# Cross-attention block: turning the attention probabilities through DRAM instead of on TensorE, with a deeper software pipeline

## The chip, the cores and the metric

One core of one Trainium2 chip runs the whole program. The metric is the time of one execution on the device in microseconds. The engines are PE (TensorE), DVE (VectorE), ACT (ScalarE), POOL (GpSimd) and SP (SyncE, which here only issues DMAs); each works through its own list of instructions in order and waits on semaphores that other engines raise.

## What is computed

64 batches, each with `x` and `ctx` of 128 x 512 in float32. A first attention works over channels (128) and positions (512), a second one has 16 heads of 32 channels over 128 queries and 128 keys, and a two-layer MLP follows. Cut to what matters:

```python
def _L0(x_c, x_s, Wn, bn, Wm, bm, Wl, bl, Wo, bo):
    Mn = _conv1x1(Wn, bn, _inorm(x_c)); Mm = _conv1x1(Wm, bm, _inorm(x_s))
    A = softmax(einsum('bct,bcs->bts', Mn, Mm), axis=-1)          # 512 x 512 per batch
    Mo = einsum('bcs,bts->bct', _conv1x1(Wl, bl, x_s), A)
    return _conv1x1(Wo, bo, Mo) + x_c
def _L1(h, enc, mask, ...):
    x = layer_norm(h, ln1_w, ln1_b)
    q, k, v = heads(x @ q_w + q_b), heads(enc @ k_w + k_b), heads(enc @ v_w + v_b)
    attn = softmax(where(mask, einsum('bhqd,bhkd->bhqk', q, k) * scale, min), axis=-1)
    hidden = merge(einsum('bhqk,bhkd->bhqd', attn, v)) @ cproj_w + cproj_b + h
    y = gelu(layer_norm(hidden, ln2_w, ln2_b) @ fc_w + fc_b) @ proj_w + proj_b
    return hidden + y
```

## The kernel before

The program has two passes. `attention_pass` computes both attentions and writes `hidden` to DRAM; `mlp_pass` then reads it. The change touches the first pass only.

Every float32 product is done in three passes of float32r (`three_passes`): each operand is split into an upper half (`..._hi`, by ACT or DVE) and a lower half (`..._lo`, a subtraction on DVE or POOL).

`attention_pass` is a software pipeline in *slots*. In slot `s` each engine runs `slot(s)`, which works on several batches at once: `b0` is batch s, `b1` batch s-1, and so on, and `ahead` batch s+1. Slots -1 to 5 and the last ones are written out; those between run in a loop of four slots a turn (`slots`, L389). The order of work on an engine is the order in which its `slot` is written, by hand, and so is the PSUM bank of each product (L376 to L384). Nothing is scheduled by a program.

What one slot does before, by the names used below, in PE's order (L922 to L1043):

- M (2 x 3 products of 512 columns): the two 1x1 convolutions of b0. A turn: 16 transposes of 128 x 128 (`turn`, L900) of the first attention's matrix of b1.
- QK half 0, S0 (scores of the first attention, b0), QK half 1. QK is the keys' projection in even slots and the queries' in odd ones, for a pair of batches (`project_pair`).
- U (b1); then the **probabilities' turn**: 16 transposes of the second attention's probabilities of b4, `probs[:, r, c, :]` into banks 2 to 5 (L995); ACT copies the four banks to `pT` (L630).
- OUT0 (b1), whose result with the residual becomes `x1` on DVE (L811); S1, the masked scores of the second attention (b3, L1016 and L1021); PV, values times `pT` (b4, L1029); V (b1); XN, four transposes of `x1n` (b1); C, the output projection (b4), which DVE adds to `x1b` as `hid` (L848).

Beside PE: DVE takes maxima and sums (L745, L762, L741), lower halves (L713, L751) and the biases of `kT` and `qT` (L727, L734). ACT takes exponentials (L609, L641) and copies. POOL normalises the probabilities (L567) and takes small powers and lower halves (L547 to L560). SP issues all DMAs in its own order (L465 to L493), each behind the wait written ahead of it; `blocks` is `ctx` loaded in four pieces to 32 partitions each, so that DVE's transpose of 32 x 32 blocks (L787) gives the full transpose of `ctx`.

Of the kernel before, what the change touches and what calls it, by code (L numbers as in the profile page):

```python
# [18 lines left out]
ALU = mybir.AluOpType  # L19
# [74 lines left out]
class Handover:  # L94
# [6 lines left out]
    def __init__(self, nc, stack):  # L101
# [20 lines left out]
        self.hid = sb("hid", [P, 2, 512])  # L122
# [65 lines left out]
def attention_pass(nc, x, ctx, mask, w, hidden, mlp):  # L188
# [8 lines left out]
    with ExitStack() as stack:  # L197
# [13 lines left out]
        probs = mlp.rows[:, 1, :, :].rearrange("p r (c n) -> p r c n", n=P)  # L211
# [11 lines left out]
        x_ctx_in = sb("x_ctx_in", [P, 2, 2, T])  # L223
        x_in, ctx_in = x_ctx_in[:, 0, :, :], x_ctx_in[:, 1, :, :]
# [3 lines left out]
        normed = sb("normed", [P, 2, T])  # L228
# [12 lines left out]
        x1n = sb("x1n", [P, D])  # L241
# [6 lines left out]
        mlp_raw = (x_ctx_in[:].rearrange("p s u t -> p (s u) t"),  # L248
# [90 lines left out]
        qT_set = sem("qT_set")  # L339
        k_done = sem("k_done")  # L340
        kT_set = sem("kT_set")
# [8 lines left out]
        pT_turned = sem("pT_turned")  # L350
        pT_copied = sem("pT_copied")
# [24 lines left out]
        M_BANK = (4, 5)  # L376
        AT_BANK = S1_BANK = (0, 1, 2, 3)
        QK_BANK = (6, 1)
        S0_BANK = (4, 5, 7, 0)
        U_BANK = XN_BANK = 6  # L380
        PT_BANK = (2, 3, 4, 5)
        OUT0_BANK = C_BANK = 7
        PV_BANK = 4
        V_BANK = 5  # L384

        FIRST, LOOPED, LAST = -1, 6, B + 3
# [29 lines left out]
        def _(sp):  # L416
# [5 lines left out]
            def load(e):  # L422
                if e.has_before(2):
                    after(normed_set, (e + -2).nth(2, 2))
                u = e.parity
                sp.dma_start(x_in[:, u, :], x[e.number]).then_inc(x_loaded[u], 16)
                sp.dma_start(ctx_in[:, u, :], ctx[e.number]).then_inc(ctx_loaded[u], 16)
# [24 lines left out]
            for i, n in enumerate(("bn", "bm", "bl", "bo")):  # L452
                sp.dma_start(bias0[:, i:i + 1], w[n].rearrange("(p a) -> p a", a=1)).then_inc(small_in, 16)
            load(Batch(0, 1, B))
            load_weight(K_W)
# [8 lines left out]

            def slot(s):  # L465
                e = s + 2
                if e.exists() and e.has_before(2):
                    load(e)
# [7 lines left out]
                e = s + -2  # L476
# [8 lines left out]
                if s.first():  # L485
                    load_weight(C_W)
                e = s + 1
                if e.exists() and e.has_before(1):
                    load_blocks(e)
                e = s + -4  # L490
                if e.exists():
                    after(hid_set, e.nth(1, 1))
# [24 lines left out]
        def _(pool):  # L517
# [14 lines left out]
            def slot(s):  # L532
# [8 lines left out]
                if b0.first():  # L541
                    lower_halves(K_W)
# [830 lines left out]
```

## Time and profile before

| | us |
|---|---|
| median of 3 runs (3113.08 to 3116.71) | 3116.62 |
| the profiled execution's own time | 3114.79 |
| its span, first to last instruction | 3112.8 |
| attention pass, to the last `hid` | some 1704 of it |
| one slot in the middle of the pass | 25.23, and 25.4 to 25.5 on the mean of four |

The profiled execution took 2 us outside its span, and it lies 1.8 us below the median. The MLP pass (the rest) is the same code in both kernels. The timeline views are read as follows: the start in us from the span's start, how long the row's instructions took together, the engine, the line of the kernel and the operation, what was written from what, and how many instructions are merged; in square brackets, how long the engine stood idle before it and whose end it then followed. Successive instructions of DVE and ACT overlap by some 0.06 to 0.1 us, so the distance of two starts, not the duration, is what an instruction takes of its engine.

### The profile page before, as it was taken

The numbers are of one execution on the slowest core, as the hardware profiler recorded it, in microseconds if no ns is written. First come the engines' busy times: TensorE is split into PE (matmuls) and PEld (weight loads), VectorE is DVE, ScalarE is ACT, GpSimd is POOL, SyncE is SP. The second block draws the span as 40 slices with busy tenths as digits, with TensorE's granted clock in tenths as the row PEclk, the third lists the DMA queues.
The fourth block names the chain that finished last, engine by engine and source line by source line (L and its number), as shares of the span: only waits on it lengthen the run. The fifth ranks groups of instructions, "written<-read, shape, count | busy, mean of one in ns | idle before, by whom it ended". The sixth has DMA issues, their size and how long they took to land. (4 is left out here: it accounts for less than half of the span.)

```text
span 3112.8 us, 56124 instructions
## 1 busy us (share of the span) xinstructions
PE 3043.9 (98%) x19575; PEld 2582.9 (83%) x19575; DVE 1802.5 (58%) x3577; ACT 1499.1 (48%) x4210; POOL 796.0 (26%) x742
## 2 busy tenths in 40 slices
PE   6999999999999999999996999999999999999999
PEld 5888888888888888888885888888888888888887
DVE  6777777777777777777774433333333333333332
ACT  5777777777777777777774211111111111111111
POOL 4444444444444444444433100000000000000000
PEclk8999999999999999999998999999999999999999
DMA  4111111111111111111102211111110111111110
GB/s 129 45 52 56 52 52 52 52 53 55 52 52 52 52 52 52 52 52 56 58 32 81 85 31 38 40 40 40 40 40 14 40 35 33 40 40 40 40 27 14
DMA packets 232040, 149.49 MB, mean 48 GB/s; under 512 B 142912, under 2 KB 176192, under 8 KB 231872
## 3 DMA queue, kind: packets, MB, share of 16 engines
q1 hardware_dynamic: 231872, 146.91, 16.0%
q8 instruction: 147, 2.41, 0.3%
q14 instruction: 21, 0.17, 0.0%
HBM read 97.57 MB, written 33.55 MB: 42 GB/s over the span
## 5 line engine op out<-in xcount | busy, mean ns | idle before, releaser
L1218 ACT ACTIVATE gl<-pre,fc_bias 128x512 f32<-128x512 f32 x256 | 176.6, 690 | 1119.9 <-PE pre L1303 1119.9
L1257 DVE CAST hT_hi<-gl 128x512 fp32r<-128x512 f32 x256 | 109.1, 426 | 839.5 <-ACT gl L1218 839.5
L641 ACT ACTIVATE rows<-bank,negmax 128x128 f32<-128x128 f32 x1024 | 359.4, 404 | 10.2 <-DVE negmax L745 10.2
L1301 PE MATMUL pre<-yT_lo,rest_hi 128*128 128x512 f32 x768 | 298.8, 389 | 0.0
L1302 PE MATMUL pre<-yT_hi,rest_lo 128*128 128x512 f32 x768 | 298.8, 389 | 0.0
L1303 PE MATMUL pre<-yT_hi,rest_hi 128*128 128x512 f32 x768 | 298.8, 389 | 0.0
L1301 PE MATMUL acc<-rest_lo,hT_hi 128*128 128x512 f32 x768 | 298.8, 389 | 0.0
L1302 PE MATMUL acc<-rest_hi,hT_lo 128*128 128x512 f32 x768 | 298.8, 389 | 0.0
L1303 PE MATMUL acc<-rest_hi,hT_hi 128*128 128x512 f32 x768 | 298.8, 389 | 0.0
L567 POOL TENSOR_TENSOR rows<-rows,rsum 128x512 f32<-128x512 f32 x256 | 261.4, 1042 | 90.0 <-DVE rsum L741 89.2
L609 ACT ACTIVATE rows<-bank,negmax 128x512 f32<-128x512 f32 x256 | 175.0, 688 | 213.0 <-DVE negmax L762 213.0
L641 ACT ACTIVATION_READ_ACCUMULATOR rows<-bank,negmax 128x1 f32 x1024 | 250.0, 244 | 0.0
L900 PEld LDWEIGHTS bank<-ident,rows 128*128 128x128 f32 x2048 | 231.5, 140 | 20.0 <-ACT rows L641 2.6
L900 PE MATMUL bank<-ident,rows 128*128 128x128 f32 x2048 | 245.2, 273 | 2.4 <-ACT rows L641 1.8
L177 POOL TENSOR_TENSOR rstd<-ve,neghalf 128x4 f32<-128x4 f32 x16 | 16.3, 1019 | 870.0 <-DVE ve L171 870.0
L615 ACT ACTIVATE rows<-rows,rsum 128x512 f32<-128x512 f32 x256 | 164.2, 713 | 69.6 <-DVE rsum L781 69.6
L1259 DVE TENSOR_TENSOR hT_lo<-gl,hT_hi 128x512 fp32r<-128x512 f32 x256 | 177.4, 693 | 8.8
L762 DVE TENSOR_REDUCE negmax<-bank 128x1 f32<-128x512 f32 x256 | 174.8, 691 | 2.6 <-PE bank L871 2.3
L547 POOL TENSOR_TENSOR in_rstd<-in_ve,neghalf 128x2 f32<-128x2 f32 x64 | 45.3, 708 | 510.6 <-DVE in_ve L776 510.6
L560 POOL TENSOR_TENSOR normed_lo<-normed,normed_hi 128x512 fp32r<-128x512 f32 x128 | 174.5, 1385 | 2.7 <-ACT normed_hi L635 2.7
L1302 PEld LDWEIGHTS pre<-yT_hi,rest_lo 128*128 128x128 f32 x768 | 144.3, 188 | 30.1
L1301 PEld LDWEIGHTS acc<-rest_lo,hT_hi 128*128 128x128 f32 x768 | 144.4, 188 | 29.9
(160 smaller groups left out, 7926.7 us busy)
## 6 DMA issues: line engine op xcount, KB each, us to landing
x_ctx_in<-in_x SPq DMA_DIRECT2D x64, 256.0 KB, 2.6
x_ctx_in<-in_ctx SPq DMA_DIRECT2D x64, 256.0 KB, 2.9
blocks<-in_ctx SPq DMA_DIRECT2D x256, 64.0 KB, 1.9
small<-in_x SPq DMA_DIRECT2D x64, 256.0 KB, 3.5
hidden<-hid SPq DMA_DIRECT2D x64, 256.0 KB, 2.0
rows<-hidden SPq DMA_DIRECT2D x16, 1024.0 KB, 5.5
out<-rows SPq DMA_DIRECT2D x64, 256.0 KB, 2.1
stage<-y SPq DMA_DIRECT2D x240, 64.0 KB, 2.1
```

Of the source, the lines that this page charges most:

```text
L560: pool.tensor_tensor(normed_lo[:, i, :], normed[:, i, :], normed_hi[:, i, :].bitcast(F32), ALU.subtract).then_inc(normed_lo_set, 1)
L567: pool.tensor_tensor(probs[:, r, :, :], probs[:, r, :, :], rsum1[:, r, :].unsqueeze(2).to_broadcast([P, 4, P]), ALU.mult).then_inc(probs_s ...
L609: act.activation(A_cols[:, t, :, :, :], bank[S0_BANK[t]][:].rearrange("p (d c x) -> p d c x", d=4, x=32), ACT.Exp, bias=negmax0[:, t:t + 1 ...
L615: act.activation(A[:, t, :], A[:, t, :], ACT.Identity, scale=rsum0[:, t:t + 1]).then_inc(a_scaled, 1)
L641: act.activation(probs[:, r, c, :], by_chunk(S1_BANK[r])[:, c, :], ACT.Exp, bias=negmax1[:, r, c:c + 1], accum_out=sum1[:, r, c:c + 1]).th ...
L762: dve.tensor_reduce(negmax0[:, t:t + 1], bank[S0_BANK[t]][:], AX_X, ALU.max, negate=True).then_inc(max0_set, 1)
L900: last = pe.transpose(out[:, c * P:(c + 1) * P], src(c), ident[:])
L1218: act.activation(gl[:, i % 2, :], pre[i % 2][:], ACT.Gelu_apprx_tanh, bias=mlp.fc_bias[:, i:i + 1]).then_inc(gelu_done, 1)
L1259: dve.tensor_tensor(hT_lo[:, i % 2, :], gl[:, i % 2, :], hT_hi[:, i % 2, :].bitcast(F32), ALU.subtract).then_inc(hT_lo_set, 1)
L1301: pe.matmul(out, a_hi, b_lo, start=first, stop=False)
L1302: pe.matmul(out, a_lo, b_hi, start=False, stop=False)
L1303: return pe.matmul(out, a_hi, b_hi, start=False, stop=last)
```

## The change

- The probabilities' turn leaves PE. The 16 transposes and ACT's four copies are gone. ACT's exponentials write `probs` in another order of columns: first the block `d` of 32 keys, then head row `r`, chunk `c` and the key within the block. POOL normalises one `r` at a time, in two calls of two.
- SP writes `probs` to a DRAM tensor `p_turn` in two halves (`write_probs`, each 512 KB in pieces of 1 KB) and reads it back in four DMAs (`read_probs`, each 256 KB in pieces of 2 KB to 32 partitions of `p_blocks`). DVE's block transpose (`turn_probs`, four calls of 128 x 512) then makes `pT`.
- The pipeline is one slot deeper: S1 works on b4, PV and C on b5, V and XN on b2; there are 70 slots in place of 69.
- The order of every engine and the banks are new. A slot on PE is now: S1, PV, V, M, XN, C, QK half 0, A turn, S0, U, QK half 1, OUT0. S1 waits for the bias of QK half 1 of the slot before it (`qT_set[1]`, `kT_set[1]`), which DVE adds after the four `turn_probs`.
- The bias of QK half 0 moves from DVE to ACT (two activations of 256 columns). `x1n` shares its memory with `x1`, the loads of `x` and `ctx` have one buffer instead of two, `hid` too.

The diff, cut to its core:

```diff
+        p_blocks = sb("p_blocks", [P, 4, T])
+        p_turn = nc.dram_tensor("p_turn", [P, 4, T], F32, kind="Internal").ap()
...
-        FIRST, LOOPED, LAST = -1, 6, B + 3
+        S1_BANK = (7, 3, 6, 4)
+        S0_BANK = (3, 6, 4, 7)
...
+        FIRST, LOOPED, LAST = -1, 6, B + 4
...
+            def write_probs(e, half):
+                if half == 0 and e.has_before(1):
+                    after(pT_set, (e + -1).nth(4, 4))
+                after(probs_set, e.nth(4, 2 * half + 2))
+                cols = slice(256 * half, 256 * (half + 1))
+                sp.dma_start(p_turn[:, :, cols], probs_flat[:, :, cols]).then_inc(p_written, 16)
+
+            def read_probs(e):
+                after(p_written, e.nth(32, 32))
+                for d in range(4):
+                    sp.dma_start(p_blocks[32 * d:32 * (d + 1), :, :],
+                                 p_turn[:, d, :].rearrange("(q p) n -> p q n", p=32)).then_inc(p_blocks_in, 16)
...
+                def turn_probs(r):
+                    if b4.exists():
+                        if r == 0:
+                            dve.wait_ge(p_blocks_in, b4.nth(64, 64))
+                        dve.transpose(pT[:, r, :, :].rearrange("p c (q b) -> p c q b", b=32),
+                                      p_blocks[:, :, r * P:(r + 1) * P].rearrange("p q (c b) -> p c q b", b=32))\
+                           .then_inc(pT_set, 1)
...
+                maximum0(2)
+                maximum0(3)
+                turn_probs(0)
+                if b0.exists():
+                    dve.wait_ge(exp0_done, b0.nth(4, 4))
+                    if b1.exists():
+                        dve.wait_ge(a_scaled, b1.nth(4, 4))
+                    dve.reciprocal(rsum0[:], sum0[:]).then_inc(rsum0_set, 1)
                 if b1.exists():
                     dve.wait_ge(u_hi_set, b1.nth(1, 1))
                     lower(u_lo[:], bank[U_BANK][:], u_hi[:], u_lo_set)
+                turn_probs(1)
+                turn_probs(2)
+                turn_probs(3)
+                second = bank[QK_BANK[1]][:].rearrange("p (c n) -> p c n", n=2 * P)
...
+                if s.parity == 0 and b4.exists() and b3.exists():
+                    pe.wait_ge(qT_set[1], b4.pair_nth(1, 1))
+                if s.parity == 1 and b3.exists() and b2.exists():
+                    pe.wait_ge(kT_set[1], b3.pair_nth(1, 1))
...
-                if b4.exists():
-                    for r in range(4):
-                        pe.wait_ge(probs_set, b4.nth(4, r + 1))
-                        if r >= 2 and b0.exists():
-                            pe.wait_ge(exp0_done, b0.nth(4, r - 1))
-                        turn(bank[PT_BANK[r]], lambda c: probs[:, r, c, :], pT_turned)
```

DVE, end of one slot and start of the next, in the loop. Before (`negmax` of L745 are the maxima of S1, `x` is `x1`):

```order
L802 TENSOR_SCALAR normed<-x_ctx_in,in_mv,in_rstd 128x512
L713 TENSOR_TENSOR u_lo<-bank,u_hi 128x512 [waits u_hi_set]
L810 REGISTER_ALU [waits x1b_set,out0_done]
L811 SCALAR_TENSOR_TENSOR x<-bank,out_bias,small 128x512 [waits x_res_loaded]
L814 BN_STATS x_stats<-x 128x6 [waits x1_set]
L817 BN_AGGR x_mv<-x_stats 128x2 [waits x1_stat]
L819 TENSOR_SCALAR x_ve<-x_mv 128x1 [waits x1_aggr]
L745 TENSOR_REDUCE negmax<-bank 128x4 [waits s1_done]
```

And the same place now:

```order
L763 STREAM_TRANSPOSE y<-p_blocks 128x512 [waits p_blocks_in]
L881 RECIPROCAL rsum<-sum 128x4 [waits a_scaled,exp0_done]
L750 TENSOR_TENSOR u_lo<-bank,u_hi 128x512 [waits u_hi_set]
L763 STREAM_TRANSPOSE y<-p_blocks 128x512 x3
L896 TENSOR_TENSOR qT<-bank,q_bias 128x512 [waits q_done]
L901 REGISTER_ALU [waits out0_done]
L902 SCALAR_TENSOR_TENSOR x<-bank,out_bias,small 128x512 [waits x_res_loaded]
L905 BN_STATS x_stats<-x 128x6 [waits x1_set]
L791 BN_AGGR x_mv<-x_stats 128x2 [waits x1_stat]
```

Between the maxima of S0 and `x1` DVE now has four transposes of `p_blocks`, the first behind the wait for the four reads, and the bias of `qT` (in the other parity `kT`) behind them.

SP in one slot of the loop, from the store of `hid` on. Before:

```order
L493 DMA hidden<-hid 128x512
L419 REGISTER_ALU
L426 ISA [waits normed_set]
L426 DMA x_ctx_in<-in_x 128x512
L427 DMA x_ctx_in<-in_ctx 128x512
L475 DMA small<-in_x 128x512 [waits x1_set]
L483 REGISTER_ALU [waits mask_set]
L483 DMA mask_u<-in_mask_BxS_bf 4x128
L439 DMA blocks<-in_ctx 32x4x128 [waits ctxT_turned]
```

And now, from the first write to the read (ahead of it stand the loads of `small` and the mask, behind it those of `blocks`):

```order
L474 DMA p_turn<-rows 512x1x256 [waits probs_set]
L506 ISA [waits hid_set]
L506 DMA hidden<-hid 128x512
L423 REGISTER_ALU
L474 DMA p_turn<-rows 512x1x256 [waits probs_set]
L423 REGISTER_ALU
L430 ISA [waits normed_set]
L430 DMA x_ctx<-in_x 128x512
L431 DMA x_ctx<-in_ctx 128x512
L423 REGISTER_ALU
L479 DMA p_blocks<-p_turn 32x4x512 [waits p_written]
L479 DMA p_blocks<-p_turn 32x4x512 x3
```

The second write waits for POOL's fourth normalisation, the read for both writes' landing, and the loads of the next `x` and `ctx` stand between them.

## Rows read from the trace of the kernel before

**Rows 1.** Stages view: length; busy PE, PEld, DVE, ACT, POOL; clock, DMA share, GB/s.

```profile
900.00:1100.00 200.00, 198.78 (x1649) 172.56 (x1648) 154.69 (x315) 152.88 (x472) 84.56 (x80) 1.00 0.16 54
```

**Rows 2.** PE's timeline over one slot, from S1 to S1.

```profile
903.86 1.91 PE L900 MATMUL bank<-ident,rows 128*128 128x128 f32 x16
905.53 0.48 PE L869 MATMUL bank<-u_lo,small_hi 128*128 128x512 f32 x1
...
906.40 0.40 PE L1016 MATMUL bank<-mask_less,masked_bf 1*128 1x512 bf16 x4
...
931.63 0.40 PE L1016 MATMUL bank<-mask_less,masked_bf 1*128 1x512 bf16 x4
```

**Rows 3.** DVE's timeline over the same slot.

```profile
906.60 0.75 DVE L811 SCALAR_TENSOR_TENSOR x<-bank,out_bias,small 128x512 f32<-128x512 f32 x1 [1.21 <-PE bank L871]
...
908.52 1.28 DVE L745 TENSOR_REDUCE negmax<-bank 128x4 f32<-128x512 f32 x2
909.72 0.68 DVE L713 TENSOR_TENSOR outT_lo<-bank,outT_hi 128x512 fp32r<-128x512 f32 x1
910.31 0.54 DVE L829 TENSOR_SCALAR x1n<-x,x_mv,x_rstd 128x512 f32<-128x512 f32 x1
...
915.63 0.66 DVE L713 TENSOR_TENSOR xnT_lo<-bank,xnT_hi 128x512 fp32r<-128x512 f32 x1
...
917.69 2.47 DVE L713 TENSOR_TENSOR at_lo<-bank,at_hi 128x512 fp32r<-128x512 f32 x4
...
924.27 0.69 DVE L768 BATCH_NORM_STATS2 in_stats<-x_ctx_in 128x6 f32<-128x512 f32 x1
...
926.06 0.18 DVE L781 RECIPROCAL rsum<-sum 128x4 f32<-128x4 f32 x1
...
927.15 0.70 DVE L787 STREAM_TRANSPOSE small_t<-blocks 128x512 f32<-128x512 f32 x1
```

**Rows 4.** ACT's timeline: the first exponential of S1, and what follows the sixteenth.

```profile
909.26 0.36 ACT L641 ACTIVATE rows<-bank,negmax 128x128 f32<-128x128 f32 x1
...
914.75 0.70 ACT L654 ACTIVATE xnT_hi<-bank 128x512 fp32r<-128x512 f32 x1
```

**Rows 5.** POOL's timeline: the fourth normalisation of the probabilities.

```profile
915.79 1.04 POOL L567 TENSOR_TENSOR rows<-rows,rsum 128x512 f32<-128x512 f32 x1 [0.54 <-DVE rsum L741]
```

**Rows 6.** DVE's and POOL's timelines in another slot of the loop.

```profile
171.98 1.68 DVE L829 TENSOR_SCALAR x1n<-x,x_mv,x_rstd 128x512 f32<-128x512 f32 x1
...
170.82 2.55 POOL L560 TENSOR_TENSOR normed_lo<-normed,normed_hi 128x512 fp32r<-128x512 f32 x2
```

**Rows 7.** SP's timeline: the store of `hid`, in the slot of rows 2.

```profile
915.86 0.38 SPq L493 DMA_DIRECT2D hidden<-hid  x1
```

**Rows 8.** The page's last part: DMAs, KB each, us from issue to landing.

```profile
x_ctx_in<-in_x SPq DMA_DIRECT2D x64, 256.0 KB, 2.6
...
hidden<-hid SPq DMA_DIRECT2D x64, 256.0 KB, 2.0
rows<-hidden SPq DMA_DIRECT2D x16, 1024.0 KB, 5.5
```

**Rows 9.** Issues of `k_w`; DMA view, 9 to 13 us; first and last piece's landing.

```profile
6.40 1.85 SPq L447 DMA_DIRECT2D stage<-in_L_xattn_k_w  x4
...
GB/s 225 225 246 225 205 266 205 184 225 184 225 205 164 266 205 164 225 184 225 307 266 225 225 266 225 184 246 225 164 266 225 164 266 184 164 169 184 210 220 128
...
stage<-in_L_xattn_k_w SPq DMA_DIRECT2D x1, 256.0 KB, 4.1
...
stage<-in_L_xattn_k_w SPq DMA_DIRECT2D x1, 256.0 KB, 6.3
```

**Rows 10.** PE's timeline: first product of M of batches 5 and 63.

```profile
125.94 0.39 PE L869 MATMUL bank<-normed_lo,small_hi 128*128 128x512 f32 x1
...
1601.76 0.39 PE L869 MATMUL bank<-normed_lo,small_hi 128*128 128x512 f32 x1
```

**Rows 11.** DVE's timeline: the last `hid` of the pass.

```profile
1702.81 0.69 DVE L848 TENSOR_TENSOR hid<-bank,stage 128x512 f32<-128x512 f32 x1 [3.52 <-PE bank L871]
```

More of the change, by code:

```diff
@@ L486, in slot @@
                     load_weight(C_W)
+                if (s + -4).exists():
+                    write_probs(s + -4, 0)
+                e = s + -5
+                if e.exists():
+                    after(hid_set, e.nth(1, 1))
+                    sp.dma_start(hidden[e.number], hid[:]).then_inc(hid_stored[e.parity], 16)
+                if (s + -4).exists():
+                    write_probs(s + -4, 1)
+                e = s + 2
+                if e.exists() and e.has_before(2):
+                    load(e)
+                if (s + -4).exists():
+                    read_probs(s + -4)
                 e = s + 1
@@ L489, in slot @@
                     load_blocks(e)
-                e = s + -4
-                if e.exists():
-                    after(hid_set, e.nth(1, 1))
-                    sp.dma_start(hidden[e.number], hid[:, e.parity, :]).then_inc(hid_stored[e.parity], 16)
             def load_for_mlp():
@@ new lines, in slot @@
+                sum1_reciprocal(0)
+                if b5.exists():
+                    dve.wait_ge(outT_hi_set, b5.nth(1, 1))
+                    lower(flat(outT_lo), bank[PV_BANK][:], flat(outT_hi), outT_lo_set)
+                if b5.exists() and not b4.exists():
+                    first_group()
+                if b2.exists():
+                    dve.wait_ge(v_done, b2.nth(1, 1))
+                    if not b2.has_before(1):
+                        dve.wait_ge(vecs_in, 16 * 6)
+                    dve.tensor_tensor(v_sb[:, b2.quarter, :], bank[V_BANK][:], v_bias[:], ALU.add).then_inc(v_set, 1)
@@ new lines, in slot @@
+                if b2.exists():
+                    pe.wait_ge(x1n_set, b2.nth(1, 1))
+                    turn(bank[XN_BANK], lambda c: x1n[:, c * P:(c + 1) * P], xnT_turned)
+                if b5.exists():
+                    if b5.first():
+                        pe.wait_ge(w_lo_set[C_W], 4)
+                    if b2.exists():
+                        pe.wait_ge(v_set, b2.nth(1, 1))
+                    elif b6.exists():
+                        pe.wait_ge(hid_set, b6.nth(1, 1))
+                    project(bank[C_BANK], outT_hi, outT_lo, C_W, cproj_done)
@@ new lines, in slot @@
+                if b0.exists():
+                    pe.wait_ge(m_lo_set, b0.nth(2, 2))
+                    for t in range(DC):
+                        if b4.exists() and t < 3:
+                            pe.wait_ge(exp1_done, b4.nth(16, 4 * t + 8))
+                        if t == 3 and keys:
+                            pe.wait_ge(kT_set[0], b2.pair_nth(2, 2))
+                        if t == 3 and queries:
+                            pe.wait_ge(qT_set[0], b3.pair_nth(2, 2))
+                        cols = slice(t * P, (t + 1) * P)
+                        three_passes(bank[S0_BANK[t]][:], m_hi[:, 0, cols], m_lo[:, 0, cols], m_hi[:, 1, :],
+                                     m_lo[:, 1, :]).then_inc(s0_done, 1)
@@ new lines, in slot @@
+                if b1.exists():
+                    pe.wait_ge(ctxT_lo_set, b1.nth(1, 1))
+                    for j in range(DC):
+                        pe.wait_ge(at_lo_set, b1.nth(4, j + 1))
+                        last = three_passes(bank[U_BANK][:], ctxT_hi[:, j, b1.parity, :], ctxT_lo[:, j, b1.parity, :],
+                                            at_hi[:, j, :], at_lo[:, j, :], j == 0, j == DC - 1)
+                    last.then_inc(u_done, 1)
+                qk(1)
+                if b1.first():
+                    prepare_q_bias()
```

508 lines of the change are left out of this document (234 added, 274 removed).

## Prediction

> **What bounds the kernel now.** I read the stages view first, then the timelines of each engine over one slot. In the middle of the attention pass PE is busy 198.8 of 200 us at full clock (2.4 GHz), DVE 154.7, ACT 152.9, POOL 84.6 [rows 1]. PE's timeline has no gap in the slot: S1 starts at 906.40 and again at 931.63, so a slot is 25.23 us of PE's work [rows 2]. DVE has 5 us to spare in it, and its idle times end with PE's results, not the other way round [rows 3]. The first product of M of batch 5 starts at 125.94, that of batch 63 at 1601.76: 58 slots, 25.445 us each on average [rows 10]; a turn of the loop costs the extra. So PE is the bound, and what leaves PE is a gain as long as nothing else needs a whole slot. The reader has to look for a chain that goes round once a slot, because that is what the change builds.
>
> **What the change takes away.** The probabilities' turn takes PE from 903.86 to 905.53, 1.67 us a slot [rows 2]. All else on PE stays, so its floor is 25.23 - 1.67 = 23.56 us. ACT loses four copies of about 0.5 us and gains two short activations; it has 23% to spare, and the sixteen exponentials, 909.26 to 914.75, 5.5 us, are the same number in the same form [rows 4]. I take ACT at nothing; its cover is the slack that rows 1 show.
>
> **What it adds on DVE.** Four block transposes, each like the one of `ctx`, 0.70 us, of which 0.62 is its own time [rows 3]: 4 x 0.62 = 2.48. The bias of QK half 0 leaves: -0.6. DVE goes from 19.5 us a slot (154.7 of 200, of 25.23) to 21.4. That fits 23.56 on its own, but not with waits in the middle.
>
> **The chain that goes round.** S1 of the next slot waits for the bias of QK half 1 on DVE. That stands behind the four transposes, the first of which waits for the read of `p_blocks`. The read waits for the write, the write for POOL's fourth normalisation, this for the fourth reciprocal on DVE, and DVE reaches it only after all that it has to do since the last bias. Everything is one instruction list, so I add it up from bias to bias (start to start, from the distances of rows):
>
> 1. DVE from the bias to the fourth reciprocal. Bias 0.61 (an add of 0.69 [rows 11], the next starting 0.08 before its end); `x1` to `x_ve` 1.92; two maxima 1.20; `x1n` 0.46; two maxima 1.20; `outT_lo` 0.59; V's add 0.61; statistics of `x` and `ctx` 1.79; `xnT_lo` and two `m_lo` 2.06; `hid` 0.61; three reciprocals 0.3 [rows 3]. Sum 11.35. ACT's exponentials are done by then: 5.5 us plus `outT_hi`, `xnT_hi` and two `m_hi` put in between, some 8 us from the first maximum, which is 3.1 us in.
> 2. The reciprocal and its semaphore 0.22, POOL's normalisation 1.04 [rows 5].
> 3. SP sees it 0.23 us later (`hid` ends 915.63, the store is issued 915.86 [rows 3, 7]).
> 4. The second write, 512 KB in pieces of 1 KB. No row shows it. A store of 256 KB lands in 2.0; 768 KB more of a load cost 5.5 - 2.6 = 2.9, so 256 KB cost 0.97 [rows 8]. I take 2.9. Lower end 2.6; upper end 5.5, if the 512 pieces count and not the bytes (`rows<-hidden` has 512). SP then sees the landing: 0.2, an estimate from step 3.
> 5. The read, 1 MB in four DMAs to 32 partitions each. `rows<-hidden`, 1 MB to 128 partitions, takes 5.5 [rows 8]. But the loads of `k_w` have the very form of this read: in 9 to 13 us, when they and `v_w` arrive, the DMA engines are full and move some 214 GB/s, and the first piece, issued at 6.40, landed at 10.5, the last, issued 1.4 later, at 14.1: 1.2 us per 256 KB [rows 9]. An idle queue gives the first piece in some 2.9 (2.6 plus what the slower rate adds), so 2.9 + 3 x 1.2 = 6.5. Lower end 5.5, upper end 7.7 (6.40 to 14.1, behind other loads). I take 6.5, since the form is the same.
> 6. DVE: four transposes 2.48, the reciprocal of the first softmax 0.1 and `u_lo` 0.61, which stand among them, and 0.05 to start.
>
> Sum: 11.35 + 0.22 + 1.04 + 0.23 + 2.9 + 0.2 + 6.5 + 2.48 + 0.1 + 0.61 + 0.05 = 25.68 us.
>
> 7. POOL and DVE in each other's way. In rows 6 `x1n` takes 1.68 us in place of 0.54 [rows 3], and starts inside POOL's `normed_lo`: it waits until POOL lets go. In the new order `x1n` falls 3.7 us after the bias, and POOL by then has done `x1b` and the small power and is at `ctxT_lo`, a subtraction of the form of `normed_lo` (2.55 for two, so 1.3 [rows 6]); I charge 0.6, about half of it. And `normed`, an instruction of the same form as `x1n`, is issued just before POOL's fourth normalisation can start: 0.2 more. Ends: 0, and 2.1 (a full wait on both sides). The Trainium skill, "SBUF — State Buffer", section "Who interferes with whom", says that a VectorE instruction in a two-port mode and a GpSimd instruction exclude each other for their whole length. By that rule, the trace agrees.
>
> Together 25.68 + 0.8 = **26.5 us a slot**, against 25.445: +1.05. Over 58 slots +61 us. PE's 1.67 us are given back and more: it will stand idle some 2.9 us a slot, ahead of S1 and OUT0.
>
> The Trainium skill bears on step 5 on both sides. "SBUF — State Buffer", section "Door 1: The DMA port swizzle", says that a transfer to partitions 0 to 31 reaches 8 of 16 ports, with an asymptote of 218 GB/s; the 214 of rows 9 agree. The same page's section "The DMA setup-cost knee" fits a transfer as 2 us plus its bytes at 436 GB/s, which would be an estimate of 4.4 us for the read and 24.4 us for the slot; rows 8 (5.5) and 9 speak against it here.
>
> **Head and tail.** At the head slots 1 to 3 lack V, XN and S1 (some 3.6 us of PE's work), part of it hidden by other waits: -4, estimated. At the tail the attention pass before ends at 1702.81 + 0.7, 101.8 us after M of batch 63 [rows 10, 11]. After, slots 64 and 65 are held by the same chain (24.5 us each for want of PE's and DVE's other work), the last two batches have the probabilities' buffer and DVE's transposes between them, and each runs the chain in full: from S1 of slot 66 to the last `hid` some 52 us (an estimate: the two slots' exponentials and maxima, 9.8 for the bounce and 2.5 for transposes, nearly twice, and PV and C). 26.5 + 24.5 + 24.4 + 52 = 127, less 5.1 since M stands 5.1 us into its slot (S1, PV and V ahead of it, estimated): 122, +20. Together +16.
>
> The sum against the profile's own execution: 3114.8 + 61 + 16 = 3192. Its time lies 1.8 below the median of the runs, so against the median it is **3194**.
>
> **Rivals.**
>
> A. The bounce is hidden (the other side). If the read runs at the full rate (5.5, -1.0), the write lands in 2.6 (-0.3) and the locks of step 7 don't fall as I lay them (-0.8), the chain is 24.4 us, and 3116.6 - 58 x 1.05 + 16 = 3072. The point from which it decides: the slot is 25.17 us, that is 1.3 us less than my sum. For it: each of the three is possible by itself, and the sum has twenty terms. Against: rows 9 are of the same form. If it were still quicker, DVE would be next: `u_lo` waits for U, then three transposes and the bias end 0.5 us after PE's OUT0, 24.05 us, 3052. Chance 0.20.
>
> B. No change that can be told, the slot between 25.06 and 25.28: 0.06. "Faster" and "slower" begin 0.2%, 6 us, from 3116.6, about what a measurement of this kernel can tell from no change.
>
> C. The chain as I have it, slot 25.3 to 27.6: 0.62.
>
> D. Slower still: the write costs by its 512 pieces (5.5, +2.6), which puts the slot at 29 and the time at 3116.6 + 58 x 3.65 + 22 = 3350, or PE's clock falls to 1.2 GHz in its gaps. Against the clock: rows 1 show it full with PE busy all the time, and PE would still be busy 23.56 of 26.5 us; no row shows it at such a share. Against the write: stores land sooner than loads of the same size [rows 8]. Chance 0.12.
>
> E. The change isn't what it says (it reads nothing late, the waits fall elsewhere): with PE at its floor of 23.56 the time is 3116.6 - 58 x 1.89 + 16 = 3023. It needs DVE to get its blocks before 19 us into the slot, against 22.6 in my sum (22.4 behind the bias, plus the locks, less the bias itself); part of A's 0.20.
>
> **The numbers.** The forecast is C's middle, 3194. The range takes A's nearer part and C to its end: low 3065 (slot 24.3), high 3265 (slot 27.7); outside lie D and the far end of A. Faster 0.20 (A), same 0.06 (B), slower 0.74 (C and D).
>
> **What would show it.** In the profile after: S1 (L1010) starts 26.5 us apart; PE's idle time ahead of it ends with DVE's L891 or L896, or DVE's first `turn_probs` (L763) stands idle 2 to 4 us a slot for the DMA of `p_blocks`, which lands 6.5 us after its first issue. POOL's fourth normalisation ends some 12.8 us after S1's start, and the read's landing comes 9.8 after that. `x1n` (L801) takes over 1 us in most slots. A transpose keeps its 0.62. Wrong would be: no idle time ahead of L763 (rival A, and then the price of the read is the step that failed), or idle time on PE that ends with ACT or POOL, which no term above has.

## The result

The changed kernel takes 3382.96 us (median of 4 runs, 3382.19 to 3388.36) against 3116.15 us (median of 4, 3113.08 to 3116.71): ratio 1.0862, 95% interval 1.0843 to 1.0881. It is 8.6% slower. The forecast had the direction and the chain that sets the slot, and under a third of the size: 3194, at most 3265. The profiled execution has a span of 3380.4 us, 267.6 more than before.

The stages view of the same 200 us as rows 1 (length; busy PE, PEld, DVE, ACT, POOL; clock, DMA share, GB/s), and of 5 us in it:

```profile
900.00:1100.00 200.00, 176.62 (x1331) 151.01 (x1330) 149.33 (x292) 125.94 (x389) 73.18 (x68) 0.91 0.42 119
919.00:924.00 5.00, 5.00 (x70) 4.12 (x71) 4.16 (x9) 1.91 (x10) 3.02 (x3) 0.50 0.19 53
```

PE is busy 176.6 of 200 us where it was 198.8 [rows 1], and the granted clock is 0.91 where it was 1.00. The second row shows where that comes from: in 919 to 924 the clock stands at 0.50, that is 1.2 GHz. PE's timeline over one slot, to be read beside rows 2:

```profile
914.55 0.28 PE L923 MATMUL bank<-xnT_hi,qc_hi 128*128 128x256 f32 x1
916.51 0.50 PE L921 MATMUL bank<-u_lo,small_hi 128*128 128x512 f32 x1 [1.68 <-DVE u_lo L750]
...
917.08 0.40 PE L923 MATMUL bank<-u_hi,small_hi 128*128 128x512 f32 x1
918.97 0.61 PE L1010 MATMUL bank<-mask_less,masked_bf 1*128 1x512 bf16 x4 [1.49 <-DVE qT L896]
919.37 1.92 PE L1015 MATMUL bank<-kT,qT 32*128 32x128 f32 x32
921.22 1.93 PE L1024 MATMUL bank<-y,stage 128*32 128x128 f32 x32
923.08 0.80 PE L921 MATMUL bank<-first_lo,ctxT_hi 128*128 128x512 f32 x1
...
926.57 0.39 PE L921 MATMUL bank<-normed_lo,small_hi 128*128 128x512 f32 x1
...
948.55 0.61 PE L1010 MATMUL bank<-mask_less,masked_bf 1*128 1x512 bf16 x4 [1.49 <-DVE kT L891]
```

S1 starts at 918.97 and 948.55: a slot of 29.58 us. Ahead of it PE stood idle twice, 1.68 us for `u_lo` and 1.49 us for the bias (L896, in the other parity L891), with 0.97 us of work between (916.51 to the end of OUT0 at 917.48). What follows runs at half the clock until some 924.5: S1 takes 2.25 us to PV's start, PV 1.86 to V's, V 3.49 to M's. DVE's timeline of the same slot, beside rows 3:

```profile
909.80 1.28 DVE L780 TENSOR_REDUCE negmax<-bank 128x1 f32<-128x512 f32 x2
915.11 0.71 DVE L763 STREAM_TRANSPOSE y<-p_blocks 128x512 f32<-128x512 f32 x1 [4.04 <-DMA p_blocks<-p_turn]
...
916.38 1.88 DVE L763 STREAM_TRANSPOSE y<-p_blocks 128x512 f32<-128x512 f32 x3
918.19 0.65 DVE L896 TENSOR_TENSOR qT<-bank,q_bias 128x512 f32<-128x512 f32 x1
...
921.36 1.29 DVE L774 TENSOR_REDUCE negmax<-bank 128x4 f32<-128x512 f32 x2 [0.61 <-PE bank L1015]
922.57 0.54 DVE L801 TENSOR_SCALAR x<-x,x_mv,x_rstd 128x512 f32<-128x512 f32 x1
...
926.77 0.69 DVE L815 TENSOR_TENSOR stage<-bank,v_bias 128x512 f32<-128x512 f32 x1 [1.80 <-PE bank L923]
...
931.95 0.17 DVE L770 RECIPROCAL rsum<-sum 128x4 f32<-128x4 f32 x1
...
944.70 0.71 DVE L763 STREAM_TRANSPOSE y<-p_blocks 128x512 f32<-128x512 f32 x1 [4.18 <-DMA p_blocks<-p_turn]
...
947.77 0.65 DVE L891 TENSOR_TENSOR kT<-bank,vecs 128x512 f32<-128x512 f32 x1
```

Here the reader sees the chain of the prediction go round, from bias (918.19) to bias (947.77), and three waits in it: 0.61 us for S1 ahead of the maxima, 1.80 us for V ahead of its add (L815), 4.18 us for the read of `p_blocks` ahead of the first `turn_probs` (4.04 in the slot before). POOL's and SP's links of it:

```profile
932.20 1.25 POOL L561 TENSOR_TENSOR rows<-rows,rsum 128x512 f32<-128x512 f32 x1 [1.07 <-DVE rsum L770]
```

```profile
933.55 0.53 SPq L474 DMA_DIRECT2D p_turn<-rows  x1
934.42 0.34 SPq L430 DMA_DIRECT2D x_ctx<-in_x  x1
...
936.87 1.76 SPq L479 DMA_DIRECT2D p_blocks<-p_turn  x4
```

The first product of M of batches 5 and 63 in PE's timeline, and the last `hid` in DVE's, beside rows 10 and 11:

```profile
134.59 0.39 PE L921 MATMUL bank<-normed_lo,small_hi 128*128 128x512 f32 x1
```

```profile
1834.06 0.39 PE L921 MATMUL bank<-normed_lo,small_hi 128*128 128x512 f32 x1
```

```profile
1972.38 0.68 DVE L845 TENSOR_TENSOR hid<-bank,stage 128x512 f32<-128x512 f32 x1
```

From 134.59 to 1834.06 it is 58 slots of 29.30 us, against 25.445 [rows 10]. So 223.6 us of the loss are in these slots, 8.7 ahead of them (134.59 against 125.94) and 37.3 behind them (139.0 us to the end of the last `hid` against 101.7 [rows 10, 11]).

The slot, link by link, against the sum of the prediction:

| from bias to bias | predicted | measured | |
|---|---|---|---|
| bias to fourth reciprocal | 11.95 (0.6 of it a lock) | 13.76 | +1.81 |
| reciprocal, POOL's fourth normalisation | 1.46 (0.2 a lock) | 1.50 | +0.04 |
| to SP's issue of the second write | 0.23 | 0.10 | -0.13 |
| write, and SP seeing it | 3.10 | 3.32 | +0.22 |
| read, to the first `turn_probs` | 6.50 | 7.83 | +1.33 |
| transposes, `rsum0`, `u_lo`, to the bias | 3.24 | 3.07 | -0.17 |
| slot | 26.5 | 29.58 | +3.1 |

Two links carry the miss, the first and the read. The first took 13.76 us in place of the 11.35 that DVE's instructions alone came to: the 2.41 more are the two waits for PE, 0.61 and 1.80.

### The profile page after: what moved, and what is told of

It reads as the page before. It is cut to its first block and busy times, and to the rows that moved or that the text cites. A ratio compares the mean times of both kernels' runs of the same rounds, so it can differ in the third digit from the quotient of the medians.

```text
span 3380.4 us, 55060 instructions
## 1 busy us (share of the span) xinstructions
PE 3083.9 (91%) x18551; PEld 2590.9 (77%) x18551; DVE 1936.8 (57%) x3769; ACT 1439.3 (43%) x4082; POOL 807.2 (24%) x742
## 5 line engine op out<-in xcount | busy, mean ns | idle before, releaser
L1270 ACT ACTIVATE gl<-pre,fc_bias 128x512 f32<-128x512 f32 x256 | 176.6, 690 | 1116.9 <-PE pre L1355 1116.9
L561 POOL TENSOR_TENSOR rows<-rows,rsum 128x512 f32<-128x512 f32 x256 | 278.8, 1089 | 339.9 <-DVE rsum L770 339.9
L763 DVE STREAM_TRANSPOSE y<-p_blocks 128x512 f32<-128x512 f32 x256 | 165.8, 687 | 288.8 <-DMA p_blocks<-p_turn 288.8
L573 POOL TENSOR_TENSOR stage<-x,cproj_bias 128x512 f32<-128x512 f32 x64 | 81.2, 1269 | 818.4 <-DVE x L902 818.4
L636 ACT ACTIVATION_READ_ACCUMULATOR rows<-bank,negmax 128x1 f32 x1024 | 241.2, 236 | 0.0
L750 DVE TENSOR_TENSOR at_lo<-bank,at_hi 128x512 fp32r<-128x512 f32 x256 | 169.3, 683 | 50.3 <-ACT at_hi L684 50.3
L774 DVE TENSOR_REDUCE negmax<-bank 128x4 f32<-128x512 f32 x256 | 164.1, 683 | 39.4 <-PE bank L1015 39.1
L594 POOL TENSOR_TENSOR normed_lo<-x_ctx,normed_hi 128x512 fp32r<-128x512 f32 x128 | 172.4, 1367 | 10.0 <-ACT normed_hi L670 10.0
L1355 PEld LDWEIGHTS acc<-rest_hi,hT_hi 128*128 128x128 f32 x768 | 144.2, 188 | 30.1
```

Source lines behind the costliest of these rows:

```text
L561: pool.tensor_tensor(probs[:, :, r, :, :], probs[:, :, r, :, :], rsum1[:, r, :].unsqueeze(1).unsqueeze(3).to_broadcast([P, 4, 4, 32]), ALU ...
L594: pool.tensor_tensor(normed_lo[:, i, :], normed[:, i, :], normed_hi[:, i, :].bitcast(F32), ALU.subtract).then_inc(normed_lo_set, 1)
L636: act.activation(probs[:, :, r, c, :], by_chunk(S1_BANK[r])[:, c, :].rearrange("p (d b) -> p d b", b=32), ACT.Exp, bias=negmax1[:, r, c:c ...
L750: dve.tensor_tensor(out, psum, hi.bitcast(F32), ALU.subtract).then_inc(done, 1)
L763: dve.transpose(pT[:, r, :, :].rearrange("p c (q b) -> p c q b", b=32), p_blocks[:, :, r * P:(r + 1) * P].rearrange("p q (c b) -> p c q b" ...
L1270: act.activation(gl[:, i % 2, :], pre[i % 2][:], ACT.Gelu_apprx_tanh, bias=mlp.fc_bias[:, i:i + 1]).then_inc(gelu_done, 1)
```

## The experiments

The theory after the result: the chain is as forecast, but (1) PE's idle time halves its clock, so that S1 and V come late for DVE in the middle of the chain, some 2.4 us, and (2) the read costs 1.2 to 1.3 us more than forecast. Its rivals: the clock is a symptom that costs nothing, since PE has time to spare; and the read is slow by its form, or by its neighbours on the DMA engines. A run here is one execution unless it says otherwise; executions of one kernel differ by up to 0.4%. The kernel before gave 3114.75 beside the first four, 3111.62 beside the next four, and 3112.61 (median of 7) beside the last three.

### 1. Does the clock cost anything?

```diff
+                if b1.exists() and b5.exists():
+                    for _ in range(7):
+                        pe.matmul(bank[OUT0_BANK][:], ctxT_hi[:, 0, b1.parity, :], at_hi[:, 0, :], start=True, stop=True)
                 if b1.exists():
                     pe.wait_ge(u_lo_set, b1.nth(1, 1))
...
+                if b1.exists() and b6.exists():
+                    pe.wait_ge(exp0_done, b1.nth(4, 4))
+                    for _ in range(6):
+                        pe.matmul(bank[S1_BANK[0]][:], ctxT_hi[:, 0, b2.parity, :], at_hi[:, 0, :], start=True, stop=True)
                 if s.parity == 0 and b4.exists() and b3.exists():
                     pe.wait_ge(qT_set[1], b4.pair_nth(1, 1))
```

> The changed kernel plus 13 useless matmuls of 512 columns a slot in PE's two idle times: 7 ahead of OUT0's wait for u_lo, 6 ahead of S1's wait for the bias. They fill 2.9 of the 3.2 us in which PE stands idle at 914.8 to 919.0. Theory 'clock' (the granted clock falls to half after the idle times, so that S1, PV and the first quarter of V take 2.4 us longer, and DVE waits 0.6 us for S1 and 1.8 us for V in the middle of its chain): slot 29.5 - 2.4 = 27.1 us, time 3383 - 60 x 2.4 = about 3240, granted clock 1.00. Rival 'the bounce sets it alone' (DVE's chain does not depend on how fast PE goes): the time stays at 3375 to 3390 although the clock is full.

Measured: 3339.23 us, clock 0.973. More work on PE made the kernel 44 us faster. PE's timeline of it, over a good slot and the turn of the loop behind it:

```profile
901.89 0.39 PE L1014 MATMUL bank<-mask_less,masked_bf 1*128 1x512 bf16 x4
...
903.11 1.08 PE L1028 MATMUL bank<-y,stage 128*32 128x128 f32 x32
904.12 0.50 PE L921 MATMUL bank<-first_lo,ctxT_hi 128*128 128x512 f32 x1
...
929.11 0.39 PE L1014 MATMUL bank<-mask_less,masked_bf 1*128 1x512 bf16 x4
...
955.80 0.50 PE L921 MATMUL bank<-u_lo,small_hi 128*128 128x512 f32 x1 [2.28 <-DVE u_lo L750]
...
959.50 2.92 PE L995 MATMUL bank<-at_hi,ctxT_hi 128*128 128x512 f32 x6 [2.73 <-issue]
962.35 0.61 PE L1014 MATMUL bank<-mask_less,masked_bf 1*128 1x512 bf16 x4
```

The slot is 27.22 us (901.89 to 929.11), as expected, S1 takes 1.22 us to PV's start and PV 1.01 to V's, and DVE's maxima and V's add follow what stands ahead of them without a wait. The read is unchanged at 7.65 us, and two of four slots are of this length (median 27.2, where it was 29.4). In one of four, where the loop turns, PE stands 2.28 us for `u_lo` and then 2.73 us with "issue", so for nothing that the profile shows, ahead of the second lot of fillers; the clock falls (0.50 in 959 to 962), and that slot and the next take 33.2 and 28.3 us (medians 32.2 and 28.3). These two are some 80 us more than ordinary slots over the 13 turns; without them the time would be some 3260, an estimate, beside the 3240 expected. In the changed kernel such a stop may lie inside PE's idle time and be brought into the open by the fillers; that was not tested. So the clock theory holds for the ordinary slot (27.22 against 29.58; 2.1 us by the medians), and most of what the whole missed lies in the turns of the loop.

One thing came back that the first table shows as not paid: `x1n` takes 1.12 us here,

```profile
904.86 1.12 DVE L801 TENSOR_SCALAR x<-x,x_mv,x_rstd 128x512 f32<-128x512 f32 x1
905.90 1.28 DVE L774 TENSOR_REDUCE negmax<-bank 128x4 f32<-128x512 f32 x2
...
907.76 0.68 DVE L815 TENSOR_TENSOR stage<-bank,v_bias 128x512 f32<-128x512 f32 x1
```

and 0.54 in the changed kernel (922.57 above), where DVE's wait for S1 had let POOL all but finish its own piece:

```profile
921.40 1.27 POOL L580 TENSOR_TENSOR ctxT_lo<-small_t,ctxT_hi 128x512 fp32r<-128x512 f32 x1
```
The lock of 0.6 us that the prediction charged is real, but a wait on PE covered it.

### 2. What makes the read slow?

Four runs change the read alone. "Read" is from SP's first issue to the first `turn_probs` that waited for it, median of the 57 to 64 slots; in the changed kernel 7.65 us.

The loads of the next `x` and `ctx` behind the read:

```diff
-                e = s + 2
-                if e.exists() and e.has_before(2):
-                    load(e)
                 if (s + -4).exists():
                     read_probs(s + -4)
+                e = s + 2
+                if e.exists() and e.has_before(2):
+                    load(e)
```

> The changed kernel with SP's loads of the next x and ctx (512 KB) moved behind the four reads of p_blocks. Theory 'neighbours' (the read takes 7.7 us from its first issue and not 6.5 because x and ctx, issued 2.5 us ahead of it, share the DMA engines with it): read 6.5 us, slot -1.2, time about 3310. Rival 'form' (32 partitions a DMA set the rate): read still 7.4 to 7.8 us, time 3375 to 3390.

Measured: 3352.1 us, read 7.51 us. The read is hardly shorter, so the rival holds for it; the time lies between the two ranges. The 31 us gained are 0.5 us a slot (S1 comes every 28.52 us on average, where it came every 29.02); some 0.35 of them lie in the two DMAs (the read 0.14, the write 0.2: 921.20 to 924.32 in one slot). In DVE's waits, over the whole run, the wait ahead of the read's first turn falls by 26.3 us (288.8 to 262.5) and that for S1 (L774) by 9.1 (39.1 to 30.0).

The same read, cut by groups of rows and not by blocks of partitions:

```diff
-                for d in range(4):
-                    sp.dma_start(p_blocks[32 * d:32 * (d + 1), :, :],
-                                 p_turn[:, d, :].rearrange("(q p) n -> p q n", p=32)).then_inc(p_blocks_in, 16)
+                for q in range(4):
+                    sp.dma_start(p_blocks[:, q, :],
+                                 p_turn[32 * q:32 * (q + 1), :, :].rearrange("p d n -> d p n")).then_inc(p_blocks_in, 16)
```

> The changed kernel with the same 1 MB read back by another cut: four DMAs that each go to all 128 partitions (one group q of 32 queries' rows each) in place of four that each go to 32 partitions. Same pieces of 2 KB, same bytes. Theory 'form': the read falls from 7.7 to about 5.5 us (as the load of 1 MB of hidden), slot -2.1, time about 3255. Rival 'neighbours': the read stays at 7 us or more, time 3350 to 3390.

Measured: 3707.44 us, read 12.91 us. Both theories were wrong. The stages view of this run, in the middle of a read, and of the changed kernel in the middle of one:

```profile
914.00:917.00 3.00, 0.00 (x0) 0.00 (x0) 0.00 (x0) 0.00 (x0) 0.00 (x0) 0.94 0.28 107
```

```profile
910.00:912.00 2.00, 2.00 (x11) 1.69 (x10) 1.07 (x2) 1.54 (x6) 0.00 (x0) 1.00 1.04 267
```

The DMA engines are busy to 0.28 and move 107 GB/s; in the changed kernel's read they are busy throughout and move two and a half times as much (the end of the loads of `x` and `ctx` is part of it: in 912 to 914 it is about twice as much, 217 and 199 GB/s). The outermost dimension of these DMAs counts 4 on the DRAM side (the four `d`), and 0.28 of 16 engines is a little over four. The Trainium skill, "DMA: Bandwidth & Descriptors", section "Why a DMA increments its semaphore by 16 and not by 1", gives the rule: a DMA runs on the largest number of engines up to 16 that divides its outermost dimension on both sides. The trace agrees, with 0.28 beside the 0.25 of the rule.

The next run takes that fault out. It reads to 128 partitions with 128 rows outermost, in the same pieces of DRAM as the changed kernel reads, which puts the rows in the wrong places (the right probabilities are left out):

```diff
-                                 p_turn[32 * q:32 * (q + 1), :, :].rearrange("p d n -> d p n")).then_inc(p_blocks_in, 16)
+                                 p_turn[:, q, :]).then_inc(p_blocks_in, 16)
```

> The changed kernel with the read in four DMAs of 256 KB that each go straight to all 128 partitions (row k of p_turn to partition k), so that 128 rows are there to be shared among the DMA engines; the data lands in the wrong places, and the second attention is computed from it: that part of the result is left out. Same 512 pieces of 2 KB as the changed kernel. Theory 'form' (a piece takes 84 ns and not 160 where 128 partitions are written, and the cut by groups of the run before was slow only because four rows at a time kept 4 of 16 DMA engines busy): the read lands in 5.3 to 5.8 us, slot -2 to -4 with the clock's share, time 3150 to 3270. Rival 'any read of this tensor is slow at this place': 7 us and more, time above 3350.

Measured: 3257.11 us, read 6.4 us. The form costs 1.25 us, less than expected. And with the loads behind it as well:

> The changed kernel, read back in four DMAs to 128 partitions each (rows in the wrong places, so the right probabilities are left out), and the loads of x and ctx behind it. From the first issue to the first turn_probs the read took 7.65 us in the changed kernel, 7.5 with the loads behind it, 6.4 with the 128 partitions. Theory 'each adds its part': 5.5 us here (the price of 1 MB of hidden) once both are gone, time about 3190. Rival 'neighbours cost nothing in either form': 6.3 us, time 3235 to 3260.

Measured: 3186.38 us, read 5.74 us. Both parts are there, and they don't add: the sum of the two (1.25 and 0.14) would leave 6.26 us. As measured, the loads of `x` and `ctx` cost the read 0.65 us where it goes to 128 partitions and 0.14 us where it goes to 32. The waits view (what was waited for, us in total, times, longest) of the changed kernel and of the last two:

```profile
DVE y L763 <- DMA p_blocks<-p_turn: 288.8, 64, 11.8
DVE stage L815 <- PE bank L923: 89.6, 62, 2.3
```

```profile
DVE y L763 <- DMA p_blocks<-p_turn: 200.8, 64, 10.3
DVE stage L815 <- PE bank L923: 60.1, 49, 2.3
```

```profile
DVE y L763 <- DMA p_blocks<-p_turn: 162.3, 64, 9.8
```

The first two kernels differ by 88 us in the wait for the read, and by another 29.5 in the wait for V (L815): the clock's share shrinks with the idle time ahead of S1. Together that is 117.5 of the 126 us gained.

### 3. Where the bias stands

```diff
+                second = bank[QK_BANK[1]][:].rearrange("p (c n) -> p c n", n=2 * P)
...
+                                      ALU.add).then_inc(qT_set[1], 1)
                 turn_probs(0)
...
                 turn_probs(3)
-                second = bank[QK_BANK[1]][:].rearrange("p (c n) -> p c n", n=2 * P)
...
-                                      ALU.add).then_inc(qT_set[1], 1)
```

> The changed kernel with DVE's bias of QK half 1 moved ahead of the four turn_probs; it then falls into DVE's idle time before the read lands. S1 no longer waits for the turns, only PV does. Theory 'the place of the bias': DVE's 0.6 us leave the chain, S1 starts right behind OUT0 and some 1.1 us earlier against the turns, so V's add too: slot -1.1 to -2.4 (the latter if the clock stays up), time 3240 to 3320. Rival 'only the bounce counts': -0.6 x 60, 3347.

Measured: 3282.0 us, slot 27.3: 101 us from moving one instruction of 0.61 us. The time lies in the range of the theory and far from the rival's 3347. But the move does more than shorten the chain. DVE and PE in one slot of this run:

```profile
895.00 0.69 DVE L879 TENSOR_TENSOR kT<-bank,vecs 128x512 f32<-128x512 f32 x1 [3.80 <-PE bank L923]
```

```profile
897.00 0.76 PE L921 MATMUL bank<-u_lo,small_hi 128*128 128x512 f32 x1 [2.04 <-DVE u_lo L750]
```

DVE now stands idle for the last product of QK half 1 and no longer for the read: over the whole run it waits for the read 12 times, 37.3 us in all, where it was 64 times and 288.8 us. So the bounce is off the chain that sets an ordinary slot; what goes round is PE's own work, QK half 1 to the bias, the first turn and `u_lo` on DVE, and back to OUT0. PE stands idle once, 2.04 us, and the clock is 0.51 in 897 to 900 even so. With `rsum0` and `u_lo` moved ahead of the transposes too:

> The changed kernel with the bias of QK half 1, the reciprocal of the first softmax and u_lo all moved ahead of the four turn_probs on DVE: behind the read only the transposes and x1 stay. Against the run with the bias alone moved (3282, slot 27.3): 0.7 us leave the chain, OUT0 no longer waits. Theory 'sum of DVE behind the read': slot 26.6, time 3240. Theory 'the clock does the rest' (one idle time in place of two, of 3 us): clock below 0.95 and slot above 27, time 3265 to 3290.

Measured: 3228.94 us, slot 26.4, clock 0.99 in 900 to 1100 (0.976 in the whole). Slot and time are those of the sum theory, but not for its reason: DVE waits for the read 6 times in the whole run, and 3.16 us a slot for QK half 1, and OUT0 still waits.

```profile
900.41 0.69 DVE L884 TENSOR_TENSOR qT<-bank,q_bias 128x512 f32<-128x512 f32 x1 [3.16 <-PE bank L923]
```

PE's idle times in this kernel:

```profile
901.82 0.50 PE L921 MATMUL bank<-u_lo,small_hi 128*128 128x512 f32 x1 [1.45 <-DVE u_lo L750]
...
904.21 1.08 PE L1024 MATMUL bank<-y,stage 128*32 128x128 f32 x32 [0.21 <-DVE y L763]
...
910.22 0.66 PE L952 MATMUL bank<-ident,x 128*128 128x128 f32 x4 [0.61 <-DVE outT_lo L750]
```

They are 1.45, 0.21 and 0.61 us with work between, which with the 23.56 us of PE's work is 25.8 of the 26.4 us, and the clock stays up; in the changed kernel 1.68 and 1.49 us with 0.97 between brought it down, and in the run before this one 2.04 us in one piece did.

### 4. What was PE's turn worth before?

```diff
-                        turn(bank[PT_BANK[r]], lambda c: probs[:, r, c, :], pT_turned)
+                        pe.transpose(bank[PT_BANK[r]][:, 0:P], probs[:, r, 0, :], ident[:]).then_inc(pT_turned, 1)
```

> The kernel before with 12 of the 16 transposes of the probabilities left out (one of 128 columns a bank stays), so that three quarters of that turn, and the right probabilities with it, are missing; all else, ACT's copies too, stays. Theory 'PE is the bound before': PE's 1.67 us a slot fall to 0.5, slot 25.4 - 1.2 = 24.2, time 3117 - 60 x 1.2 = 3045. Rival 'another engine stands right behind PE': 3080 or more.

Measured: 3107.61 us, 4 us less than the kernel before beside it. The rival was right. The waits view says why:

```profile
PE bank L869 <- DVE u_lo L713: 69.3, 64, 2.5
```

PE now waits 1.08 us a slot for `u_lo`. Between U and OUT0 lie ACT's `u_hi` and DVE's `u_lo`, and the transposes were what PE did meanwhile. PE had no gap in the profile before, and yet the 1.2 us taken from it were worth 0.06 a slot (4 us over 64).

### 5. The bounce in two halves

```diff
-            def read_probs(e):
-                after(p_written, e.nth(32, 32))
+            def read_probs(e, half):
+                after(p_written, e.nth(32, 16 * half + 16))
+                cols = slice(256 * half, 256 * (half + 1))
                 for d in range(4):
-                    sp.dma_start(p_blocks[32 * d:32 * (d + 1), :, :],
-                                 p_turn[:, d, :].rearrange("(q p) n -> p q n", p=32)).then_inc(p_blocks_in, 16)
+                    sp.dma_start(p_blocks[32 * d:32 * (d + 1), :, cols],
+                                 p_turn[:, d, cols].rearrange("(q p) n -> p q n", p=32)).then_inc(p_blocks_in[half], 16)
...
                     write_probs(s + -4, 0)
+                    read_probs(s + -4, 0)
...
                         if r == 0:
-                            dve.wait_ge(p_blocks_in, b4.nth(64, 64))
+                            dve.wait_ge(p_blocks_in[0], b4.nth(64, 64))
+                        if r == 2:
+                            dve.wait_ge(p_blocks_in[1], b4.nth(64, 64))
```

> The changed kernel with the bounce cut in two: the first half of the columns (heads' rows 0 and 1) is read back as soon as its own write has landed, four DMAs of 128 KB, and the second half likewise; the first two turn_probs wait for the first half only, the others for the second. Order on DVE and PE unchanged. Theory 'the read of 1 MB is the longest link' (half of it comes off the chain: the second read of 512 KB lands some 4.4 us after its issue in place of 7.7; the gaps on PE shrink, the clock recovers its 2 us): slot 25 to 25.7 us, time 3100 to 3180. Rival 'twice as many pieces cost as much as half the bytes save' (1024 pieces of 1 KB in place of 512 of 2 KB): the last read still lands 6 us or more after its issue, time above 3250.

Measured: 3081.65 us, 30 us under the kernel before beside it and under the theory's range too. The second read's last piece lands 4.2 us after its first issue, and DVE waits for a read 18 times in the whole run; its waits for S1 and V in the middle are gone from ordinary slots; most slots take 24.0 us. Then DVE's order:

```diff
                 turn_probs(0)
+                turn_probs(1)
...
-                turn_probs(1)
                 turn_probs(2)
```

> The kernel with the bounce cut in two (3082), and DVE's order around it changed: turn_probs 0 and 1, then the reciprocal of the first softmax and u_lo, then turn_probs 2 and 3 and the bias. The second transpose then fills the two waits for ACT (0.30 and 0.31 us at 907.4 and 907.9) that stand between the first and u_lo. Theory 'DVE's own list is now the slot': 0.6 us leave it, the slot goes from 24.0 to 23.6, where PE's work ends, time 3050 to 3065. Rival 'the second read comes too late': turn_probs 2 waits for it, time 3080 to 3110.

Measured, 4 runs: 3077.33 us, ratio to before 0.9884 (0.9865 to 0.9903). That is no difference from the run before that can be told: the slots stay at 23.7 to 24.1, and DVE now waits for the second read in nearly every one,

```profile
DVE y L767 <- DMA p_blocks<-p_turn: 62.6, 65, 5.0
```

where the run before it had 35.3 us in 18 times. So the rival's mechanism was at work, at a smaller price than its range. With the loads of `x` and `ctx` behind the second read:

> The same as the run beside it, and the loads of the next x and ctx moved behind the second read. If the few long slots (26 to 28.8 us, two in each 14) come from the second read standing behind these loads: 10 to 30 us less than the run beside it. If the loads have nothing to do with them: within 8 us of it; if x and ctx now come late for DVE's statistics: more.

Measured, 4 runs: **3058.34 us, ratio 0.9831 (0.9810 to 0.9853)**, 1.7% under the kernel before. The 19 us came, but not from where I looked for them: behind the head four slots of 26.0 to 27.7 us are still there (four of 26.0 to 28.6 in the run beside it), and the ordinary ones went from 24.0 to 23.7.

```profile
900.00:1100.00 200.00, 197.91 (x1647) 171.23 (x1647) 188.26 (x366) 153.81 (x498) 92.41 (x87) 1.00 0.43 139
```

```profile
DVE y L767 <- DMA p_blocks<-p_turn: 34.7, 16, 5.2
```

PE is busy 197.9 of 200 us at full clock, and the slot is 0.1 us above the 23.56 us of PE's own work. So the order of the engines in the change can run at PE's pace; what kept it from that was the length of one chain.

## The prediction, point by point

**PE bounds the kernel before, and its floor is 23.56 us.** In the new order right: the last kernel gets to 23.7. As a price of the removed work it was wrong, as experiment 4 shows: in the old order the turn covered the latency from U to `u_lo`, and without it the slot stays at 25.2. The gap-free timeline of rows 2 told that PE was busy, not that its work was in the way. The new order puts QK half 1 into that place, which the prediction didn't see as part of what the change bought.

**The chain that goes round once a slot.** Right in all its links, in their order, and in what shows it: the idle time ahead of L763 ends with the read, PE's ahead of S1 with L891 or L896. The write (3.32 against 3.1), POOL's step (1.50 against 1.46) and the transposes (3.07 against 3.24) came out as worked out.

**Step 1, 11.35 us from the bias to the fourth reciprocal: the step that failed.** I added DVE's instructions as if nothing in the middle could be late, after having written that DVE's work doesn't fit with waits in the middle. Measured it was 13.76 us, 2.41 more, all of it DVE's waits for PE. S1, PV and V stand behind the same bias, and DVE's maxima and V's add behind them. At full clock there is no wait in it (experiment 1). Behind the idle times, with the clock at half until some way into V, they take 2.25 + 1.86 + 3.49 = 7.6 us in place of 1.22 + 1.01 + 2.9, and DVE waits 0.61 + 1.80 us.

**The clock.** It stood only in rival D, as "in its gaps", with 0.12 and no price of its own, and was argued down because no row showed a clock at such a share of busy time. That was the wrong way to use a missing row: the sum itself forecast 2.9 us of idle time a slot (3.17 were measured), rows 1 had never seen any, and so the clock belonged in the range as an unknown with two ends. Priced by what was measured afterwards, S1, PV and V behind a fallen clock cost 2.5 us more. That puts the slot at 29.0, or 28.4 where the lock of 0.6 is hidden by it, and 3116.6 + 58 x 2.96 to 3.56 + 16 makes 3304 to 3339.

**Step 5, the read, 6.5 us.** Measured 7.83 in this slot and 7.65 in the median, at its upper end (7.7). The form was rightly recognised, since 128 partitions give 6.4. What was too low is the first piece, taken as 2.9 from a load to 128 partitions. The tile view of `p_blocks` in the changed kernel gives its pieces' landing:

```profile
DMA to landing us min/median/max: 3.8/5.2/7.2
```

The quickest takes 3.8, and the median of the first pieces is 4.0; with 3 x 1.2 behind it, as rows 9 have them, that is 7.6, and the median from first issue to last landing is 7.63. Why the first piece takes 4.0 and not 2.9 is shown in part: to 128 partitions it takes 3.3 (experiment 2, medians), and 3.15 with the loads behind it.

**Step 7, the locks.** The 0.6 for `x1n` was not paid in most slots (0.54), but paid at once when the clock's wait was gone (1.12). The 0.2 for POOL's fourth normalisation was paid: 1.25 us in place of 1.04. That the one lock was hidden under a wait that the sum lacked is luck, and made the miss smaller by 0.6 us a slot.

**Head and tail.** Forecast +16, measured +46: -4 became +8.7, +20 became +37.3. In PE's timeline the last two batches show the bounce bare, with nothing to cover it:

```profile
1909.60 0.61 PE L1010 MATMUL bank<-mask_less,masked_bf 1*128 1x512 bf16 x4 [10.07 <-DVE qT L896]
...
1939.30 1.93 PE L1024 MATMUL bank<-y,stage 128*32 128x128 f32 x32 [12.96 <-DVE y L763]
...
1963.38 1.94 PE L1024 MATMUL bank<-y,stage 128*32 128x128 f32 x32 [15.23 <-DVE y L763]
```

From 1909.60 to the end of the last `hid` it is 63.5 us and not 52; the three slots ahead took 83.6 and not 75.4; M stood 8.0 us into its slot and not 5.1. Why the head came 8.7 us later and not 4 earlier is open.

**The sum.** 58 slots at +3.86 in place of +1.05 are 163 us more, head and tail 30 more: 3387, beside the 3383 measured.

## What to carry to other kernels

Where a sum forecasts that TensorE will wait, price what the wait does to its clock on the work behind it, and look whether another engine in the chain waits for that work: here over 2 us a slot, more than the transfers were mis-sized. Cut a round trip through DRAM so that only its last part stands behind the last result: that alone took the change from 8.6% slower to some 1% faster, and with DVE's order and the loads behind the second read it was 1.7%. Or put whatever doesn't need the transfer ahead of the wait for it, which took it to 3229 us without any cut; the two together were not tried. After such a move look again at what the engine waits for: here the bounce had left the chain, and PE's own product stood in its place. An engine with no gap in its timeline is not thereby the bound; ask what latency the work you take away was covering.

## What was not expected of the hardware

- The clock fell to 0.50 behind two idle times of 1.68 and 1.49 us with 0.97 us of work between, and to 0.51 behind one of 2.04 us (experiment 3, first run), and stayed at 1.00 in the stretches around idle times of 1.45, 0.21 and 0.61 us spread over the slot.
- DMAs whose outermost dimension counts 4 on the DRAM side kept the DMA engines 0.28 busy at 107 GB/s, and 1 MB took 12.91 us in place of 7.65.
- 512 KB of loads to 128 partitions, issued ahead of a read of 1 MB, made it 0.65 us longer where the read goes to 128 partitions too (5.74 to 6.40) and 0.14 us where it goes to 32 at a time (7.51 to 7.65).
